# Late weights behind the second batch's queries, step lists of their own for the closing rounds, and the last tile's activations turned on TensorE

## The reference, cut to what matters

```python
xn, ln = layernorm(ctx, ln1_w, ln1_b), layernorm(_layernorm(x), ln2_w, ln2_b)
q = (ln @ Wq) * (1 + side) + side                  # 256 -> 1024
k, v = split(xn @ Wkv)                             # 256 -> 2048
x = x + tanh(g_xattn) * (softmax(q k^T / 8) v) @ Wout
h = gelu(act_quant(rmsnorm(_layernorm(x))) @ ternary(w1).T + b1)
x = x + tanh(g_ffn) * (act_quant(rmsnorm(h)) @ ternary(w2).T + b2)
```

## Time and profile before

| what | value |
|---|---|
| median of three runs | 1146.59 us (1146.12 to 1147.98) |
| profiled execution, its own time | 1148.09 us |
| its span | 1146.2 us |
| TensorE busy in the span | 1069.4 us (93%) |
| VectorE, ScalarE, GpSimd busy | 943.3 us, 974.0 us, 776.7 us |
| mean granted TensorE clock | 0.978 of full speed |

### The profile page before, as it was taken

One profiled execution on the slowest core, in us unless ns is written; L12 is line 12 of the kernel. 1 busy time (PEld: TensorE's weight loads), 2 busy tenths in 40 slices (PEclk: granted clock), 3 DMA queues, 4 the chain that ended last, 5 costly groups with the idle time before them and its releaser, 6 DMA issues.

```text
span 1146.2 us, 32095 instructions
## 1 busy us (share of the span) xinstructions
PE 1069.4 (93%) x11890; PEld 735.4 (64%) x11890; DVE 943.3 (82%) x2108; ACT 974.0 (85%) x1866; POOL 776.7 (68%) x837
## 2 busy tenths in 40 slices
PE   3788999999999999999999999999999999999972
PEld 1455666776676676767666676776677667766650
DVE  3686788888889888888888878888988878988863
ACT  4677789999999979999999979999999979998861
POOL 3466577776767777676777666767777776777631
PEclk9899999999999999999999999999999999999975
DMA  8155745676786656778865776676667676755451
GB/s 273 50 97 91 115 87 108 125 114 113 117 137 108 103 113 124 117 108 125 119 111 110 127 115 104 112 136 101 111 126 114 117 122 111 120 107 103 105 103 30
DMA packets 418840, 129.72 MB, mean 113 GB/s; under 512 B 392480, under 2 KB 417536, under 8 KB 418688
## 3 DMA queue, kind: packets, MB, share of 16 engines
q1 hardware_dynamic: 418688, 127.68, 63.5%
HBM read 26.71 MB, written 3.67 MB: 27 GB/s over the span
## 4 chain that ended last, share of the span: by engine, by line
PE 71%; ACT 9%; DMA 6%; issue 6%; POOL 3%; DVE 3%; POOLq 1%; SPq 0%; DVEq 0%; ACTq 0%
PE work L757 15%; PE work L759 14%; PE work L758 14%; PE ps_s L776 10%; DMA pt<-pn 6%; PE ps_o L757 3%; PE ps_o L759 3%; PE ps_o L758 3%; ACT prob L538 2%; PE work L839 2%; PE work L857 2%; ACT L538 2%; ACT q_f L504 2%; PE work L863 2%; PE work L830 2%
## 5 line engine op out<-in xcount | busy, mean ns | idle before, releaser
L379 POOL TENSOR_TENSOR pn<-prob,pn 112x750 f16<-112x750 f32 x256 | 399.5, 1566 | 123.1 <-ACT pn L548 111.6
L538 ACT ACTIVATE prob<-ps_s,neg_max 112x375 f32<-112x375 f32 x512 | 265.2, 573 | 16.7 <-DVE neg_max L680 13.6
L680 DVE TENSOR_REDUCE neg_max<-ps_s 112x2 f32<-112x750 f32 x256 | 237.4, 928 | 23.6 <-PE ps_s L776 23.5
L757 PE MATMUL ps_o<-v_h,pt 128*128 128x65 f16 (+1 forms) x1536 | 168.3, 195 | 18.3 <-DMA pt<-pn 14.6
L757 PE MATMUL work<-z,wkv_h 128*128 128x375 f16 x512 | 168.6, 329 | 15.2 <-DVE k_l L605 8.1
L461 ACT ACTIVATE k_h<-work 128x375 f16<-128x375 f32 x256 | 121.4, 487 | 61.2 <-PE work L759 55.6
L605 DVE SCALAR_TENSOR_TENSOR k_l<-work,k_h 128x375 f16<-128x375 f32 x256 | 136.3, 540 | 40.7 <-ACT k_h L461 40.5
L758 PE MATMUL ps_o<-v_l,pt 128*128 128x65 f16 (+1 forms) x1536 | 168.0, 193 | 0.0
L759 PE MATMUL ps_o<-v_h,pt 128*128 128x65 f16 (+1 forms) x1536 | 168.0, 194 | 0.0
L759 PE MATMUL work<-z,wkv_l 128*128 128x375 f16 x512 | 167.4, 327 | 0.0
L758 PE MATMUL work<-z,wkv_h 128*128 128x375 f16 x512 | 167.0, 326 | 0.0
(11 more groups left out here) (125 smaller groups left out, 2729.7 us busy)
## 6 DMA issues: line engine op xcount, KB each, us to landing
ctx_in<-in_ctx SPq DMA_DIRECT2D x32, 375.0 KB
pt<-pn SPq DMA_TRANSPOSE x256, 3.5
x_in<-in_x SPq DMA_DIRECT2D x32, 112.0 KB, 3.4
x_res<-in_x SPq DMA_DIRECT2D x28, 128.0 KB, 4.1
out<-y SPq DMA_DIRECT2D x28, 128.0 KB, 2.0
stage<-in_wkv SPq DMA_DIRECT2D x2, 1024.0 KB, 9.6
stage<-in_w SPq DMA_DIRECT2D x2, 1024.0 KB, 11.8
stage<-in_wq SPq DMA_DIRECT2D x1, 1024.0 KB, 9.1
```

The costliest lines, as they stand in the source:

```text
L379: g.tensor_tensor(buf[:, 1, :, 0:SK], prob[:, p % 2], buf[:, 0, :, 0:SK], ALU.subtract).then_inc(p_lo, 1)
L538: i = a.activation(prob[:, p % 2, h, :], ps_s[0:SQ, 2 * (p % 2) + h, 0:SK], ACT.Exp, bias=neg_max[:, 2 * (p % 2) + h:2 * (p % 2) + h + 1])
L680: v.tensor_reduce(neg_max[:, 2 * (p % 2):2 * (p % 2) + 2], ps_s[0:SQ, 2 * (p % 2):2 * (p % 2) + 2, 0:SK], X, ALU.max, negate=True).then_in ...
L757: t_.matmul(dst, sh, mh, start=(n == 0), stop=False)
```

## The change

1. `load` is split in two. The late loads now hang behind the query load of batch 1, and the SP list has ("LX", 1) ahead of ("LD", 1): the order is queries of batch 1, late weights, context of batch 1. The first residual load moves from the head of the list to behind T1 of batch 1. All opening lists are written anew; all hold the same steps as before, in another order.
2. Each engine gets a list `LAST` that it runs at the end in place of what `ORDER` would give. It begins at ("Q0", 30) on TensorE.
3. For the last tile (NT - 1) the two DMA transposes fall away. TensorE turns the quantised row (XT, 2 transposes of 128x128 float16) and the hidden row (HT, 8 of them) into a bank of PSUM, and VectorE's clips read from there.

Cut to its core (the lists' ends only):

```diff
-ORDER, FIRST = {}, {}
+ORDER, FIRST, LAST = {}, {}, {}
...
@@ FIRST["PE"] @@
-    ("ZX", 0), ("Z0", 0), ("Z1", 0), ("K0", 0), ("K1", 0), ("K2", 0), ("K3", 0), ("K4", 0),
...
+    ("Z1", 0), ("ZX", 0), ("Z0", 0), ("K1", 0), ("K2", 0), ("K0", 0), ("K3", 0), ("K4", 0),
...
@@ FIRST["DVE"] @@
-    ("BA", 0), ("BB", 0), ("BS", 0), ("WKL", 0), ("WQL", 0), ("BA", 1), ("KL0", 0), ("BB", 1),
...
+    ("BA", 0), ("BB", 0), ("BS", 0), ("WKL", 0), ("WQL", 0), ("BA", 1), ("KL1", 0), ("BB", 1),
...
@@ FIRST["SP"] @@
-    ("RS", 1), ("LD", 1), ("LX", 1), ("LX", 2), ("LD", 2), ("T0", 0), ("T1", 0), ("LD", 3),
-    ("T2", 0), ("LX", 3), ("T3", 0), ("T4", 0), ("T5", 0), ("T6", 0), ("T7", 0), ("T0", 1),
-    ("T1", 1), ("LD", 4), ("T2", 1), ("T3", 1), ("T4", 1), ("LX", 4), ("T5", 1), ("T6", 1),
+    ("LX", 1), ("LD", 1), ("LD", 2), ("LX", 2), ("T0", 0), ("T1", 0), ("T2", 0), ("LX", 3),
+    ("LD", 3), ("T3", 0), ("T4", 0), ("T5", 0), ("T6", 0), ("T7", 0), ("T0", 1), ("T1", 1),
+    ("RS", 1), ("T2", 1), ("LD", 4), ("LX", 4), ("T3", 1), ("T4", 1), ("T5", 1), ("T6", 1),
-    ("T5", 2), ("T6", 2), ("T7", 2), ("XD", 1), ("T0", 3), ("T1", 3), ("LD", 6), ("RS", 2),
-    ("T2", 3), ("T3", 3),
+    ("T5", 2), ("T6", 2), ("T7", 2), ("XD", 1), ("T0", 3), ("T1", 3), ("LD", 6), ("T2", 3),
+    ("RS", 2), ("T3", 3),
+]
+LAST["PE"] = [
...
+    ("K7", 31), ("S3", 31), ("S4", 31), ("OO0", 30), ("V02", 31), ("S5", 31), ("A4", 30), ("A5", 30),
+    ("K6", 31), ("A6", 30), ("F2", 27), ("A7", 30), ("S6", 31), ("S7", 31), ("OO1", 30), ("V01", 31),
+    ("V00", 31), ("WO", 30), ("F0", 29), ("F1", 29), ("V11", 31), ("A0", 31), ("V12", 31), ("V10", 31),
+    ("A1", 31), ("A2", 31), ("A3", 31), ("A4", 31), ("A5", 31), ("F2", 28), ("A6", 31), ("A7", 31),
+    ("OO0", 31), ("OO1", 31), ("F0", 30), ("F1", 30), ("WO", 31), ("F2", 29), ("XT", 31), ("F0", 31),
+    ("F1", 31), ("F2", 30), ("HT", 31), ("F2", 31),
+]
+LAST["ACT"] = [
...
+    ("KH6", 31), ("GE", 28), ("OH1", 30), ("VH01", 31), ("SQ", 28), ("VH00", 31), ("E6", 31), ("E7", 31),
+    ("PH6", 31), ("HR", 28), ("VH11", 31), ("VH12", 31), ("VH10", 31), ("GE", 29), ("XR", 30), ("SQ", 29),
+    ("OH0", 31), ("OH1", 31), ("HR", 29), ("GE", 30), ("SQ", 30), ("XR", 31), ("HR", 30), ("GE", 31),
+    ("SQ", 31), ("HR", 31),
+]
+LAST["DVE"] = [
...
+    ("N3", 30), ("PH5", 31), ("M6", 31), ("M7", 31), ("OT1", 30), ("HMX", 28), ("VL01", 31), ("VL00", 31),
+    ("X1", 30), ("SC2", 28), ("HE0", 29), ("PH7", 31), ("HE1", 29), ("XST", 30), ("VL11", 31), ("N0", 31),
+    ("VL12", 31), ("VL10", 31), ("N1", 31), ("SC1", 30), ("HTE", 28), ("N2", 31), ("HMX", 29), ("YE", 28),
+    ("N3", 31), ("SC2", 29), ("XTE", 30), ("OT0", 31), ("OT1", 31), ("HE1", 30), ("HE0", 30), ("X1", 31),
+    ("XST", 31), ("HTE", 29), ("SC1", 31), ("HMX", 30), ("YE", 29), ("XTE", 31), ("SC2", 30), ("HE0", 31),
+    ("HE1", 31), ("HTE", 30), ("HMX", 31), ("YE", 30), ("SC2", 31), ("HTE", 31), ("YE", 31),
+]
+LAST["POOL"] = [
...
+    ("RM2", 28), ("PL6", 31), ("PL7", 31), ("HQ", 28), ("RM1", 30), ("XQ", 30), ("RM2", 29), ("HQ", 29),
+    ("XB", 30), ("RM1", 31), ("RM2", 30), ("XQ", 31), ("HQ", 30), ("XB", 31), ("RM2", 31), ("HQ", 31),
+]
+LAST["SP"] = [
...
+    ("T3", 30), ("T4", 30), ("T5", 30), ("T6", 30), ("ST", 26), ("HD", 27), ("RS", 30), ("T7", 30),
+    ("XD", 29), ("T0", 31), ("T1", 31), ("T2", 31), ("T3", 31), ("T4", 31), ("T5", 31), ("ST", 27),
+    ("T6", 31), ("RS", 31), ("HD", 28), ("T7", 31), ("XD", 30), ("HD", 29), ("ST", 28), ("ST", 29),
+    ("HD", 30), ("ST", 30), ("ST", 31),
+]
@@ sequence @@
-    done = set(FIRST[engine])
+    done = set(FIRST[engine] + LAST[engine])
     steps = FIRST[engine] + [(name, it + off) for it in range(START, END) for name, off in ORDER[engine]
-                             if 0 <= it + off < B and (name, it + off) not in done]
+                             if 0 <= it + off < B and (name, it + off) not in done] + LAST[engine]
@@ buffers @@
-        ident = sb("ident", [P, P])
+        ident, ident_h = sb("ident", [P, P]), sb("ident_h", [P, P], F16)
@@ sync @@
-            def load(b):
-                if b == 0:
-                    return
-                sp.wait_ge(ctx_normed, b)
-                sp.dma_start(ctx_in[:], ctx[b].rearrange("(t p) d -> p t d", p=TP)).then_inc(ctx_loaded, 16)
+            def load_context(b):
+                if b > 0:
+                    sp.wait_ge(ctx_normed, b)
+                    sp.dma_start(ctx_in[:], ctx[b].rearrange("(t p) d -> p t d", p=TP)).then_inc(ctx_loaded, 16)
+
+            def load_queries(b):
+                if b > 0:
+                    sp.wait_ge(ctx_normed, b)
+                    sp.dma_start(x_in[:], x[b]).then_inc(x_loaded, 16)
                 if b == 1:
-                    sp.dma_start(gates[:, 0:1], g_x.partition_broadcast(P)).then_inc(small_in, 16)
-                    sp.dma_start(gates[:, 1:2], g_f.partition_broadcast(P)).then_inc(small_in, 16)
-                    sp.dma_start(b2_row[:], b2.partition_broadcast(P)).then_inc(small_in, 16)
-                    sp.dma_start(wout_f, wout.rearrange("(k p) n -> p k n", p=P)).then_inc(wout_in, 16)
-                    sp.dma_start(w1_f, w1.rearrange("(k p) n -> p k n", p=P)).then_inc(w1_in, 16)
-                    sp.dma_start(w2_f, w2.rearrange("(k p) n -> p k n", p=P)).then_inc(w2_in, 16)
-                    sp.dma_start(b1_row[:], b1.partition_broadcast(P)).then_inc(small_in, 16)
+                    load_late_weights()
+
+            def load_late_weights():
+                sp.dma_start(gates[:, 0:1], g_x.partition_broadcast(P)).then_inc(small_in, 16)
+                sp.dma_start(gates[:, 1:2], g_f.partition_broadcast(P)).then_inc(small_in, 16)
+                sp.dma_start(b2_row[:], b2.partition_broadcast(P)).then_inc(small_in, 16)
+                sp.dma_start(wout_f, wout.rearrange("(k p) n -> p k n", p=P)).then_inc(wout_in, 16)
+                sp.dma_start(w1_f, w1.rearrange("(k p) n -> p k n", p=P)).then_inc(w1_in, 16)
+                sp.dma_start(w2_f, w2.rearrange("(k p) n -> p k n", p=P)).then_inc(w2_in, 16)
+                sp.dma_start(b1_row[:], b1.partition_broadcast(P)).then_inc(small_in, 16)
 
...
-                if name == "XD":
+                if name == "XD" and b < NT - 1:
                     turn_quantised(b)
-                if name == "HD":
+                if name == "HD" and b < NT - 1:
                     turn_hidden(b)
                 if name == "LD":
-                    load(b)
-                if name == "LX" and b > 0:
-                    sp.wait_ge(ctx_normed, b)
-                    sp.dma_start(x_in[:], x[b]).then_inc(x_loaded, 16)
+                    load_context(b)
+                if name == "LX":
+                    load_queries(b)
                 if name == "RS":
                     load_residual(b)
@@ gpsimd @@
+            g.memset(ident_h[:], 0.0)
...
-            g.affine_select(out=ident[:], in_=ident[:], compare_op=ALU.not_equal, fill=1.0, base=0,
-                            pattern=[[-1, P]], channel_multiplier=1).then_inc(consts_ready, 1)
+            for t in (ident, ident_h):
+                i = g.affine_select(out=t[:], in_=t[:], compare_op=ALU.not_equal, fill=1.0, base=0,
+                                    pattern=[[-1, P]], channel_multiplier=1)
+            i.then_inc(consts_ready, 1)
@@ vector @@
-                if name == "XTE":
+                if name == "XTE" and b == NT - 1:
+                    dve.wait_ge(full[BANK["XT", b]], USE["XT", b])
+                    v.tensor_scalar(xqt[:].rearrange("p c q -> p (c q)"), work[:, BANK["XT", b], :].bitcast(F16)[:, 0:KC * P],
+                                    -QMAX - 1, QMAX, ALU.max, ALU.min).then_inc(evacuated[BANK["XT", b]], 1)
+                if name == "HTE" and b == NT - 1:
+                    dve.wait_ge(full[BANK["HT", b]], USE["HT", b])
+                    v.tensor_scalar(hqt[:].rearrange("p c q -> p (c q)"), work[:, BANK["HT", b], :].bitcast(F16)[:, 0:FF // P * P],
+                                    -QMAX - 1, QMAX, ALU.max, ALU.min).then_inc(evacuated[BANK["HT", b]], 1)
+                if name == "XTE" and b < NT - 1:
                     dve.wait_ge(x_turned, 16 * (b + 1))
                     v.tensor_scalar(xqt[:], xqt_r[:], -QMAX - 1, QMAX, ALU.max, ALU.min).then_inc(x_clipped, 1)
-                if name == "HTE":
+                if name == "HTE" and b < NT - 1:
                     dve.wait_ge(h_turned, 16 * (b + 1))
@@ tensor, job @@
+            wh = w.bitcast(F16)
...
+                if name == "XT":
+                    pe.wait_ge(xq_ready, b + 1)
+                    for c in range(KC):
+                        i = t_.transpose(wh[:, c * P:(c + 1) * P], xq[:, c * P:(c + 1) * P], ident_h[:])
+                if name == "HT":
+                    pe.wait_ge(hq_ready, b + 1)
+                    for c in range(FF // P):
+                        i = t_.transpose(wh[:, c * P:(c + 1) * P], hid_q[:, c * P:(c + 1) * P], ident_h[:])
...
```

(13 more changed lines are left out.)

## The result

The changed kernel takes 1134.07 us (median of 4 executions, 1131.63 to 1134.87) against 1147.24 us for the kernel before beside it (4 executions). The ratio is 0.988, 95% interval 0.9868 to 0.9892: 13.2 us faster. On another chip, run again (label after_again), it took 1130.68 us against 1147.62 us, ratio 0.9849 (0.9831 to 0.9868), 16.9 us. The forecast was 1136.0 us, 10.6 us faster, with a range of 1129.5 to 1143.5; both measured times lie in it, the second near its lower end. The profiled execution took 1134.87 us.

What follows compares the result with a forecast made beforehand. TensorE bounds the repeating round, leaving the opening, closing stretch and serial tail to win: -1.6 - 6.6 - 2.4 = -10.6 us off the median 1146.59, so 1136.0 us, range 1129.5 to 1143.5.

Steps and rivals of the forecast that it cites:

- The first wait: Opening: VectorE's wait for batch 1's queries is not removed but passes to its context, landing near 32.4 us.
- Both booked terms: Opening: +1.0 us for the later start and -2.6 us for a transpose wait near 100 us won; together -1.6 us.
- the booked +1.0 us: Opening: by 40 us the new order has one Z block and three transposes still to run; ends -1 and +3.
- Ahead of S7.31: Closing lists: between nothing and 9.7 us of TensorE idle time stays; half taken, 5.0 us.
- dense closing: Rival: the new closing lists leave nothing idle ahead of S7.31, a further -5.0 us, 1131.0 us; chance 0.15.
- that clock term: Closing: the 9.41 us of TensorE work in the half-clock stretch gets 4.1 us shorter at full clock.
- the granted clock stays at 1.00 up to WO.31: Closing, sign of being right: TensorE keeps full clock until the last output projection, WO.31.
- What is late next is tile 26's transpose: Tail: tile 26's hidden-row DMA transpose, landing at T+11.8, holds up the last tile; eats 3 of 4 us won.
- The idle time moves: Rival, closing: lists win only the clock or half the waits; 5.0 us idle grows to 10, 1141.0 us; chance 0.18.
- the turned rows gain nothing: Rival, tail: TensorE transposes and clip take 2.0 and 1.5 us, costing what the DMA does, 1137.7 us; chance 0.12.
- SyncE's new order: Rival, closing: T steps behind other loads and transposes stop A steps, two stops of 7.3 us, 1150.6 us; chance 0.06.
- Does nothing: Rival: the change doesn't do what it says; one opening load replaces another, closing lists give nothing, 1146 us; chance 0.04.

Runs made afterwards that it cites:

- e1: The changed kernel with only the new opening lists and late-load order; old closing, last tile turned by DMA: 1142.05 us, ratio 0.9966 to the kernel before.
- e4: The changed kernel with the late weights issued behind both loads of batch 1, queries and context: 1121.37 us, ratio 0.9786 to the kernel before.
- e2: The changed kernel with the opening lists and load order of before; new closing and turned rows kept: 1133.12 us, ratio 0.9887 to the kernel before.
- e10: The kernel before with 29 useless matmuls ahead of A4 to A7 of batch 31 and F0 of tile 26: 1145.87 us, ratio 0.9988.
- e3: The changed kernel with the last tile's two rows turned by DMA as before: 1134.52 us, ratio 0.99 to the kernel before.
- e5: The changed kernel with the last but one tile's hidden row turned on TensorE too: 1128.93 us, ratio 0.9836 to the kernel before.
- e6: The changed kernel with SC2 of tile 30 ahead of XTE of tile 31 in VectorE's list: 1130.99 us, ratio 0.9854 to the kernel before.
- e7: The changed kernel with 51 useless matmuls in TensorE's gaps of the tail: 1130.16 us, ratio 0.9844 to the kernel before.

## Why the prediction was right, and by how much it missed

**Opening (booked -1.6; the traces -2.3, e1 -3.6 by the medians).** The first wait moved as said, to the context's statistics, landing at 32.47 us where 32.4 was said, with TensorE idle for 7.9 us. The prediction weighed that the Trainium skill ("DMA: Bandwidth & Descriptors", Queues, rings and completion order) lets a load issued last start last; the trace agrees by 21.23 us to 32.47 us, and e4 from the other side: issued at 13.61 us, the context was waited for until 22.27 us. Part of the lateness lies ahead of the issue: SyncE could issue the context only at 21.23 us, when it was done with b1, whose issue took 4.24 us. The 2.56 us wait near 100 us is gone.

Both booked terms were right in kind; the second, -2.6 us, was too small. Three traces have the old opening (before, e2, e10), seven the new one (after, after_again, e1, e3, e5, e6, e7); mean and range in us:

| | old opening | new opening |
|---|---|---|
| first scores, S0.0, start | 44.1 (44.0 to 44.4) | 45.4 (44.0 to 46.7) |
| TensorE idle, 0 to 60 us | 27.7 (27.3 to 28.3) | 30.5 (28.9 to 31.8) |
| TensorE idle, 60 to 200 us | 10.2 (9.7 to 10.4) | 6.2 (5.8 to 6.9) |
| of it, waits for probability transposes | 5.2 (4.8 to 5.5) | 1.9 (1.5 to 2.6) |
| first X1 | 137.1 (136.5 to 137.5) | 134.3 (133.0 to 136.0) |
| X1.28 | 1031.8 (1030.5 to 1032.9) | 1028.8 (1026.7 to 1031.5) |

```profile
43.97 0.37 PE L776 MATMUL ps_s<-k_h,q_h 64*112 64x375 f16 x2 [0.46 <-POOL q_l L387]
```

```profile
45.88 0.37 PE L852 MATMUL ps_s<-k_h,q_h 64*112 64x375 f16 x2
```

The rows are of before and after. S0.0 has about the same work ahead of it in both lists (after: one Z block more and one key block less), and it starts 1.2 us later on average: the booked +1.0 us is borne out. Behind 60 us TensorE is idle 4.0 us less, of which 3.3 us are waits for probability transposes; -2.6 was booked. The steady rounds come 2.8 to 2.9 us earlier, and all of that is won by the first X1. The sum does not close in idle time alone (+2.8 - 4.0 = -1.2 us); the rest was not traced. The ranges overlap, so the -2.3 us of one pair of traces says little by itself; the means and e1's medians, -3.6 us on one chip, carry this point.

**Closing (booked -6.6; measured -9.1, e2 -10.5).** Right in kind and too small. The term that failed is "Ahead of S7.31 ... I take the half, 5.0 us": from 1030.3 to 1076 us only 0.4 us stays idle. The *dense closing* rival, given 0.15, described this stretch. The others: the last A steps keep 1.82 + 0.82 = 2.6 us (said 1.9), the hops behind them 0.45 + 0.58 = 1.0 us (said 1.3). Idle time went down by 5.6 us (said 1.5), F2.29 by 1.05, and the remaining 2.4 us of the 9.1 are work that no longer runs at half clock (said 4.1).

The size of that clock term was right where its premise held: with the clock at 1.00 it is 3.9 us (e2). The premise, "the granted clock stays at 1.00 up to WO.31", failed in the changed kernel, which has 0.94 from 1076 us, and in seven of the ten traces with its lists. With the new lists the clock is paid in full, since the idle time is the same at each; in the old order it was not, as e10 shows, where only 2.1 us of some 4 reach the end. The two errors in the changed kernel (4.0 us too much left idle, 1.7 us too much won by the clock) cancel in part. The forecast time was 1.9 us off on the first chip and the forecast gain 2.6 us (10.6 for 13.2); on the second chip they were 5.3 and 6.3 us off. So the closeness on the first chip owes something to luck.

**Tail (booked -2.4; measured -2.5, e3's counterpart 3.45).** By its steps from T: XTE ends at +5.8 (said 5.4), HE at +8.6 (8.3), tile 26's clip starts at +12.3 (11.8), SC2.31 ends at +16.4 (15.8), HQ's end to HTE's end 1.9 us (2.3, before 3.5), the whole 25.4 (25.5). The eight transposes took 1.01 us (said 1.1) and the clip of 1024 columns from PSUM 0.69 us (said 1.1). The Trainium skill ("TensorE: Matmul & The Clock Gate", Part 4: PE-mode transpose) gives 275 to 390 ns for one of bf16; here eight of float16, back to back, took 1.01 us at a granted clock of 0.50, so one took an eighth of it, 0.126 us. The trace does not bear that figure out for several in a row. "What is late next is tile 26's transpose" is shown by e5. The prediction counted 3 of 4 us as eaten by it; e3 shows why the turned X row pays all the same: it also moves SC2.30, which stands behind XTE.31, by 1.8 us.

**The rivals.** *The idle time moves* and *the turned rows gain nothing* (e3: 3.45 us) are out. *SyncE's new order* is out too: TensorE's waits in the closing rounds hold none for a probability transpose. *Does nothing* was true of the opening's first wait alone. What no case of mine held is that the first wait, left in place, is the largest thing to win: some 7 to 12 us by e4.

## What to carry to other kernels

Loads that are needed late go behind every load that the next batch waits for, not only behind one of them. To price a load that comes late, look first at the wait of the engine whose list it blocks, not at the idle time of the engine that bounds the round. In the two kernels tried here VectorE's wait was the nearer figure: 10.4 us where some 7 to 12 were won (TensorE idle: 7.9), 5.6 us where 3 to 5.5 were won (TensorE idle: 6.6). Two cases are no proof.

When the steps of an opening are reordered, count both ends: here the new opening started 1.2 us later and still won.

A half clock behind a wait is charged in full only where TensorE itself is the chain: ask whether the wait would be there at full clock too. In this serial tail, turning a tile on TensorE in place of a DMA paid 1.6 to 1.8 us for each row on the chain, and what was next was then the previous tile's transpose.
